# Eight GpSimd additions per group moved, and VectorE forms the rotation sums of three of the four groups

## The chip, the core and the metric

The kernel runs on one core of one Trainium2 chip. The metric is the device time of one execution in microseconds. Everything is float32. The median of three runs of the kernel before is 1265.38 us (1263.79 to 1267.1).

## The reference

A two-layer decoder over x of 8 batches x 256 tokens x 256 features. The first layer is attention with 16 heads, cross attention on a context of 120 rows and a mixture of 8 experts, each followed by a layer norm. The second layer, where the change lies, is a gated linear-style attention, a cross attention and a channel mix. Cut to what matters here:

```
x = _layernorm(x + L1_attn(x)); x = _layernorm(x + L1_xattn(x, ctx)); x = _layernorm(x + L1_ffn(x))

L1_attn:  xn = layernorm(x) * ln1_g + ln1_b
          q = l2norm(xn @ Wq); k = l2norm(xn @ Wk); v = xn @ Wv          # 16 heads of 16
          q = rope(q); k = rope(k)          # r1 = x1*cos - x2*sin ; r2 = x1*sin + x2*cos
          gcp = exp(clip(cumsum(-softplus(xn @ gate_w + gate_b)), -60, 50)); q *= gcp; k /= gcp + 1e-8
          p_exp = exp(p - max p) * softplus(xn @ clock_w + clock_b)      # p = xn @ p_w + p_b
          q /= cumsum(p_exp) + 1e-8; k *= p_exp
          out = softmax(causal(q @ k.T / 4)) @ v @ out_w + out_b
          x1 = out + x
          return x1 + gelu(layernorm(x1) @ mlp_w1 + mlp_b1) @ mlp_w2 + mlp_b2
```

## The kernel before

The 2048 tokens are worked in four groups (G = 4) of two batches: 512 tokens, NT = 4 tiles of 128 partitions x 256 features. The last part of the kernel, `last_layers`, is a pipeline over periods p = 0 to 3 and an end. In period p, group a = p is in the front stage (norms, projections, gates, rotation, causal attention), group r = p - 1 in the middle stage (output product, MLP), and group z = p - 2 in the rear (cross attention and channel mix). Each engine has its own list of instructions, written out by hand in order; an instruction waits only on the semaphores named before it. So an instruction that waits holds back all that stands behind it on its engine. Group 0 is alone in period 0, and its front stage is done in halves. In the trace period 0 lies at 745 to 834 us, period 1 at 834 to 925, period 2 at 925 to 1038.5, period 3 at 1038.5 to 1151.

The steps that the change touches:

- **Rotation.** VectorE `rotate` (line 2723) multiplies a 128x512 tile of queries and keys in PSUM by cos into `ra` (line 2725) and crosswise by sin into `rb` (line 2731), and signals `turning`. GpSimd adds the two (line 1572, for group 0 line 1546, 128x512) and signals `swung`. VectorE waits for `swung` (line 2974) and scales the sum by the inverse norms (line 2976), after which TensorE turns it (line 1769).
- **What VectorE does behind each tile's rotation** in periods 1 to 3: behind tile 0 the clock product (line 2940, 128x1024), behind tile 1 the product with the exponentials (line 2947), behind tile 2 four running sums (line 2672), behind tile 3 a small maximum (line 2959). Each comes right behind a drain.
- **Bias rows.** `add_rows` (line 1492) adds a bias row to four tiles on GpSimd (line 1495, 128x256 each): eight additions per group, four that fill `x1` and signal `biased0`, four in place. Before the change they stand behind the gather of the next group's expert rows and wait for `qkt`, the last of the `factors` (lines 2680 and 2683).
- **add_rest** (line 1521, 128x1024) and the clock sum (line 1567, 128x1024; line 1543 in halves for group 0), both on GpSimd.
- **Attention loop.** For every quad of heads q = 0 to 7: TensorE `scores` (line 1692), VectorE `minimum` twice (line 2746, on PSUM), ScalarE exponentials twice (line 2297), TensorE `weighted` (line 1703). Between the minimums VectorE does, for q = 1 to 4, `combine` twice (line 2625, 128x256, on the gathered expert rows of the next group) and statistics. For group 0 one `combine` follows each of the last eight minimums.

Of the kernel before, what the change touches and what calls it, by code (L numbers as in the profile page):

```python
# [8 lines left out]
ALU = mybir.AluOpType  # L9
# [11 lines left out]
NT = GT // P  # L21
# [1277 lines left out]
def last_layers(nc, dram, memory, keep):  # L1299


    with ExitStack() as ctx:
# [24 lines left out]
        HALF = NT // 2  # L1327
# [67 lines left out]
        def x(g, t):  # L1395

            return keep["x"][:, NT * g + t, :]
# [29 lines left out]
        def gates_of(g):  # L1427

            return g + 1 if g else 0
# [52 lines left out]
        def _(pool):  # L1482
# [9 lines left out]
            def add_rows(g, r, out):  # L1492

                for t in range(NT):
                    last = pool.tensor_tensor(out(t), x(g, t), brow[:, r, :], ALU.add)  # L1495
                return last
# [22 lines left out]
            def add_rest(g):  # L1519

                pool.tensor_tensor(keep["x"][:, bass.ts(g, NT), :], keep["x"][:, bass.ts(g, NT), :], x1[:, :, :], ALU.add).then_inc(biased1, 1)

            def rstd(g, n, b):

                h = slice(HALF * b, HALF * b + HALF)
                pool.wait_ge(n.stats, 2 * g + b + 1)
                pool.tensor_tensor(n.var[:, h], n.mv[:, h, 1], eps[:, h], ALU.add)  # L1527
                pool.drain()
                pool.tensor_tensor(n.inv[:, h], n.var[:, h], minus_half[:, 0, h], ALU.pow).then_inc(n.rstd, 1)  # L1529
# [8 lines left out]
            front_rstd(0, 1)  # L1538
            constants()
            pool.wait_ge(rows, NR * 16)  # L1540
            for b in range(GB):
                pool.wait_ge(uready, b + 1)
                pool.tensor_tensor(csum[:, :, batch(b)], csum[:, :, batch(b)], clog[:, :, batch(b)], ALU.add).then_inc(clogged, 1)
                for t in range(NT)[rows_of(b)]:
                    pool.wait_ge(turning, t + 1)
                    pool.tensor_tensor(firstrb[:, t, :], firstrb[:, t, :], firstra[:, t, :], ALU.add).then_inc(swung, 1)
            pool.wait_ge(vmm, NT)
            gather(1)
            pool.wait_ge(n4.normed, NT)
            pool.wait_ge(qkt, NT)  # L1550
            add_rows(0, 0, lambda t: x1[:, t, :]).then_inc(biased0, 1)
            add_rows(0, 1, lambda t: x(0, t))
            front_rstd(1, 0)
            front_rstd(1, 1)
            for p in range(1, PERIODS):
                a, r, z = stages(p)
                if z is not None:
                    pool.wait_ge(n6.turned, 2 * z + 2)
                    add_rows(z, 2, lambda t: x(z, t)).then_inc(biased2, 1)
                if r is not None:  # L1560
                    rstd(r, n5, 0)
                    rstd(r, n5, 1)
                    if z is not None:
                        add_rest(r)
                if a is not None:
                    pool.wait_ge(uready, gates_of(a) + 1)
                    pool.tensor_tensor(csum[:, :, :], csum[:, :, :], clog[:, :, :], ALU.add).then_inc(clogged, 1)
                    for t in range(NT):
                        if z is not None and t == NT - 1:
                            rstd(z, n7, 0)  # L1570
                        pool.wait_ge(turning, NT * a + t + 1)
                        pool.tensor_tensor(rb[:, t, :], rb[:, t, :], ra[:, t, :], ALU.add).then_inc(swung, 1)
                if r is not None and z is None:
                    add_rest(r)
                if z is not None:
                    rstd(z, n7, 1)
                    pool.wait_ge(n7.copied, 2 * z + 2)
                    columns = x5t[:, :, :, :].rearrange("p k b s -> p (k b) s")
                    pool.tensor_tensor(rl[:, :, :].rearrange("p k (b s) -> p (k b) s", b=GB), columns[:, :, 1:S + 1], columns[:, :, 0:S],
                                       ALU.subtract).then_inc(apart, 1)  # L1580
                if a is not None and a + 1 < G:
                    pool.wait_ge(vmm, NT * a + NT)
                    gather(a + 1)
                if a is not None:
                    pool.wait_ge(n4.normed, NT * a + NT)
                    pool.wait_ge(qkt, NT * a + NT)
                    add_rows(a, 0, lambda t: x1[:, t, :]).then_inc(biased0, 1)
                    add_rows(a, 1, lambda t: x(a, t))
                    if a + 1 < G:
                        front_rstd(a + 1)  # L1590
                if r is not None:
                    rstd(r, n6, 0)
                    rstd(r, n6, 1)
                if z is not None:
                    rstd(z, n8, 0)
                    rstd(z, n8, 1)
# [1019 lines left out]
        def _(dve):  # L2616
# [106 lines left out]
            def rotate(g, t):  # L2723

                dve.tensor_tensor((ra if g else firstra)[:, t, :].rearrange("p (h d) -> p h d", d=HALF1),
                                  bank[qk_bank(g, t)][:, :].rearrange("p (h d) -> p h d", d=HALF1),
                                  rope[:, t % 2:t % 2 + 1, 0:HALF1].to_broadcast([P, 64, HALF1]), ALU.mult)
                q4 = bank[qk_bank(g, t)][:, :].rearrange("p (h two d) -> p h two d", two=2, d=HALF1)
                r4 = (rb if g else firstrb)[:, t, :].rearrange("p (h two d) -> p h two d", two=2, d=HALF1)
                for o in range(2):  # L2730
                    last = dve.tensor_tensor(r4[:, :, o, :], q4[:, :, 1 - o, :],  # L2731
                                             rope[:, t % 2:t % 2 + 1, HALF1 * (1 + o):HALF1 * (2 + o)].to_broadcast([P, 32, HALF1]), ALU.mult)
                last.then_inc(turning, 1)

            def square_sums(g, t):

# [168 lines left out]
            for p in range(1, PERIODS):  # L2905
# [59 lines left out]
                if a is not None:  # L2965
                    dve.drain()
                    dve.wait_ge(lsum, gates_of(a) + 1)
                    dve.tensor_tensor(qfac[:, :, :], qfac[:, :, :], gsum[:, :, :], ALU.add).then_inc(qsum, 1)
                    dve.drain()
                    dve.wait_ge(ginv, gates_of(a) + 1)  # L2970
                    dve.tensor_tensor(pexps[:, :, :], pexps[:, :, :], gabs[:, :, :], ALU.mult)
                    dve.wait_ge(rnr, gates_of(a) + 1)
                    for t in range(NT):
                        dve.wait_ge(swung, NT * a + t + 1)
                        part = rb[:, t, :].rearrange("p (h d) -> p h d", d=DH1)
                        dve.tensor_tensor(part, part, rn[:, t * 32:(t + 1) * 32].unsqueeze(2).to_broadcast([P, 32, DH1]),  # L2976
                                          ALU.mult).then_inc(roped, 1)
# [251 lines left out]
```

## Time and profile before

| what | value |
|---|---|
| median of three runs | 1265.38 us |
| the profiled execution | 1264.11 us |
| its span in the trace | 1262.4 us |
| granted TensorE clock, mean | 0.961 of full |
| GpSimd busy over the span | 457.1 us (36%) |
| VectorE busy over the span | 750.2 us (59%) |

Times in the rows are microseconds from the span's start, unless marked ns. Line numbers are those of the kernel. DVE is VectorE, ACT ScalarE, PE TensorE (its matmuls), POOL GpSimd. In rows of the timeline the first number is the start, the second the time to the end of the merged instructions; a bracket holds the engine's idle time just before and what ended it.

### The profile page before, as it was taken

How to read it: one execution, taken by the hardware profiler on the slowest of the kernel's cores; microseconds unless marked ns; L12 is line 12 of the kernel's file. 1: busy time of each engine (PE TensorE's matmuls, PEld its weight loads, DVE VectorE, ACT ScalarE, POOL GpSimd, SP SyncE). 2: the span in 40 equal slices, each digit the busy share in tenths (PEclk: the TensorE clock that was granted, in tenths of full speed). 3: DMA queues.
4: the chain of work that ended last, by engine and by line, in shares of the span. 5: the costliest groups of instructions: out<-in, count | busy, mean ns of one | idle time of the engine just before them, and what ended most of it. 6: DMA issues, size and time to landing. Idle time of an engine off the chain costs nothing. (4 is left out here: it accounts for less than half of the span.)

```text
span 1262.4 us, 20442 instructions
## 1 busy us (share of the span) xinstructions
PE 1113.0 (88%) x6750; PEld 789.2 (63%) x6750; DVE 750.2 (59%) x2260; ACT 548.3 (43%) x1411; POOL 457.1 (36%) x539
## 2 busy tenths in 40 slices
PE   7899988998899798699999948579798999999996
PEld 3466455644564467599999945345565575566774
DVE  1383367236724764455556546749849885966366
ACT  1372237124612552233333317457566556744541
POOL 0151026003500575566666642503523613222022
PEclk9999999999999999699999988669999999999999
DMA  6000020020002004571111114100100100000001
GB/s 198 17 2 1 18 57 2 1 55 19 2 1 57 1 2 132 199 252 52 43 51 52 48 53 141 34 1 1 34 9 1 34 2 25 1 1 25 1 1 34
DMA packets 40228, 52.38 MB, mean 41 GB/s; under 512 B 10780, under 2 KB 33372, under 8 KB 40124
## 3 DMA queue, kind: packets, MB, share of 16 engines
q1 hardware_dynamic: 31100, 36.66, 9.1%
q0 software_dynamic: 3408, 9.31, 2.7%
q10 hardware_dynamic: 5616, 5.11, 1.2%
q8 instruction: 55, 0.90, 0.3%
q14 instruction: 49, 0.40, 0.1%
HBM read 41.76 MB, written 9.31 MB: 40 GB/s over the span
## 5 line engine op out<-in xcount | busy, mean ns | idle before, releaser
L1637 PE MATMUL bank<-words 128*128 128x256 f32 (+3 forms) x872 | 267.6, 457 | 13.3 <-DVE words L3048 2.4
L1637 PEld LDWEIGHTS bank<-words 128*128 128x128 f32 (+1 forms) x872 | 162.1, 193 | 92.4 <-issue 56.7
L419 PE MATMUL bank<-words 128*128 128x512 f32 x384 | 173.1, 602 | 8.4 <-DMA words<-in_wq 8.4
L371 POOL TENSOR_TENSOR words<-words 128x256 f32<-128x256 f32 (+1 forms) x128 | 103.4, 829 | 176.2 <-DVE words L972 176.2
L1182 PEld LDWEIGHTS bank<-words 128*128 128x128 f32 x1248 | 147.4, 194 | 3.5 <-ACT words L1216 1.6
L1182 PE MATMUL bank<-words 128*128 128x128 f32 x1248 | 147.9, 277 | 0.9 <-ACT words L1216 0.9
L754 ACT ACTIVATE words<-words 128x128 f32<-128x128 f32 (+1 forms) x256 | 113.3, 444 | 50.7 <-DVE words L967 50.7
L419 PEld LDWEIGHTS bank<-words 128*128 128x128 f32 x384 | 72.5, 193 | 90.7 <-issue 90.1
L706 ACT ACTIVATE words<-bank 128x512 f32<-128x512 f32 x48 | 28.7, 598 | 192.6 <-PE bank L419 192.6
L1231 ACT ACTIVATE words<-words 128x1024 f32 x39 | 41.1, 1057 | 145.1 <-PE bank L1182 128.4
L808 DVE COPY words<-bank 128x512 f32<-128x512 f32 x48 | 33.1, 690 | 106.3 <-PE bank L419 106.1
L963 DVE CUSTOM_DVE_ANT_0 words<-bank,words 128x128 f32<-128x128 f32 (+1 forms) x256 | 76.0, 353 | 20.4 <-PE bank L430 18.8
L1193 PE MATMUL bank<-words 128*128 x312 | 73.9, 380 | 0.7 <-DVE words L1280 0.7
L443 PE MATMUL bank<-words 128*128 128x128 f32 x384 | 55.8, 282 | 16.8 <-DVE words L983 9.1
L430 PE MATMUL bank<-words 64*128 64x128 f32 (+1 forms) x512 | 58.9, 351 | 8.6 <-DVE words L967 5.2
L1527 POOL TENSOR_TENSOR words<-words 128x2 f32<-128x2 f32 x32 | 7.0, 219 | 162.7 <-DVE words L2655 162.6
L443 PEld LDWEIGHTS bank<-words 128*128 128x128 f32 x384 | 41.7, 143 | 37.8 <-issue 26.6
L456 PE MATMUL bank<-words 128*64 128x256 f32 (+1 forms) x512 | 55.8, 337 | 10.1 <-ACT words L762 9.1
L983 DVE COPY words<-bank 128x768 f32<-128x768 f32 x64 | 59.6, 931 | 7.4 <-PE bank L443 7.4
L1138 POOL COPY words<-words 128x1024 f32 x39 | 40.3, 1035 | 60.7 <-PE bank L1182 60.7
L2297 ACT ACTIVATE words<-bank 128x768 f32<-128x768 f32 x64 | 48.9, 812 | 30.3 <-DVE bank L2746 30.3
L1193 PEld LDWEIGHTS bank<-words 128*128 128x128 f32 x312 | 56.2, 190 | 7.1 <-issue 1.1
(347 smaller groups left out, 2006.7 us busy)
## 6 DMA issues: line engine op xcount, KB each, us to landing
words<-in_w SPq DMA_DIRECT2D x8, 1024.0 KB, 9.5
y_slots<-words ACTq DMA_DIRECT2D x39, 128.0 KB, 1.7
words<-in_w SPq DMA_DIRECT2D x8, 512.0 KB, 10.1
words<-in_xt SPq DMA_DIRECT2D x4, 512.0 KB, 4.1
words<-in_x SPq DMA_DIRECT2D x4, 512.0 KB, 4.2
x_rows<-words SPq DMA_DIRECT2D x16, 128.0 KB, 1.8
words<-in_wm SPq DMA_DIRECT2D x2, 1024.0 KB, 6.6
out_x<-words SPq DMA_DIRECT2D x16, 128.0 KB, 1.8
```

Of the source, the lines that this page charges most:

```text
L371: last = pool.tensor_tensor(part, part, inv[:, j % SLOTS0, :, t:t + 1].to_broadcast([P, 2, P * (t + 1)]), ALU.mult)
L419: last = pe.matmul(bank[c % 2][:, :], w, r, start=k == 0, stop=k == KD - 1)
L430: last = pe.matmul(bank[SCORES[i % 2][n]][:, t * P:t * P + P * (t + 1)],  kt[r, m, b * S + t * P:b * S + (t + 1) * P], qt[r, m, b * S:b * ...
L443: last = pe.transpose(bank[2 + n][:, k * P:(k + 1) * P], prob[:, j % SLOTS0, n, c:c + P], ident[:, :])
L456: last = pe.matmul(bank[4 + j % 2][DH0 * n:DH0 * n + DH0, queries], v[:, 2 * b + k, h * DH0:(h + 1) * DH0], probt[:, j % 2, n, probs_of], ...
L754: last = act.activation(prob[:, i % SLOTS0, n, c], prob[:, i % SLOTS0, n, c], ACT.Exp, bias=negmax[:, i % SLOTS0, n, t:t + 1], scale=DH0 * ...
L963: dve.tensor_tensor_reduce(out=prob[:, i % SLOTS0, n, c], in0=bank[SCORES[i % 2][n]][:, c], in1=mask0[:, c], scale=1.0, scalar=-3e38, op0= ...
L983: dve.tensor_copy(probt[:, j % 2, :, :], turned).then_inc(tcopied, 1)
L1182: last = pe.matmul(bank[(BANKG, BANKV)[half][j % 2]][:, c * P:(c + 1) * P], wfix[:, j % 2, k * 2 * FF + half * FF + c * P:k * 2 * FF + hal ...
L1193: last = pe.matmul(bank[BANKY[j % 2]][:, 0:D], hidden[:, j % 2, k * P:(k + 1) * P], w2[:, bass.ds(e * W2 + k * D, D)], start=k == 0, stop= ...
L1637: last = pe.matmul(out, w, r, start=i == 0, stop=i == len(pairs) - 1)
L2297: act.activation(es[:, j % 4, :, :], pair(j % 2)[:, :, 0:CAUSAL], ACT.Exp, scale=DH1 ** -0.5).then_inc(s1e, 1)
```

## The change

Group 0: its eight bias additions move ahead of the clock sums and rotation sums; they wait for `n4.normed` alone. Groups 1 to 3: the four additions `rb + ra` leave GpSimd. VectorE makes each itself behind the tile's rotation, with a drain ahead of it, and its waits for `swung` go. The clock sum waits also for the last normalised rows of the middle group (`n5.normed`). In period 1 `add_rest` comes right behind the clock sum. The gather waits for all four `turning` signals, which the removed loop waited for until then. The eight bias additions are spread over the attention loop: two after the minimums of each of the quads q = 1 to 4.

```diff
             pool.wait_ge(rows, NR * 16)
+            pool.wait_ge(n4.normed, NT)
+            add_rows(0, 0, lambda t: x1[:, t, :]).then_inc(biased0, 1)
+            add_rows(0, 1, lambda t: x(0, t))
             for b in range(GB):
...
             gather(1)
-            pool.wait_ge(n4.normed, NT)
-            pool.wait_ge(qkt, NT)
-            add_rows(0, 0, lambda t: x1[:, t, :]).then_inc(biased0, 1)
-            add_rows(0, 1, lambda t: x(0, t))
...
                     pool.wait_ge(uready, gates_of(a) + 1)
+                    pool.wait_ge(n5.normed, NT * r + NT)
                     pool.tensor_tensor(csum[:, :, :], csum[:, :, :], clog[:, :, :], ALU.add).then_inc(clogged, 1)
-                    for t in range(NT):
-                        if z is not None and t == NT - 1:
-                            rstd(z, n7, 0)
-                        pool.wait_ge(turning, NT * a + t + 1)
-                        pool.tensor_tensor(rb[:, t, :], rb[:, t, :], ra[:, t, :], ALU.add).then_inc(swung, 1)
-                if r is not None and z is None:
-                    add_rest(r)
+                    if z is None:
+                        add_rest(r)
+                    if z is not None:
+                        rstd(z, n7, 0)
...
                 if a is not None and a + 1 < G:
                     pool.wait_ge(vmm, NT * a + NT)
+                    pool.wait_ge(turning, NT * a + NT)
                     gather(a + 1)
                 if a is not None:
                     pool.wait_ge(n4.normed, NT * a + NT)
-                    pool.wait_ge(qkt, NT * a + NT)
-                    add_rows(a, 0, lambda t: x1[:, t, :]).then_inc(biased0, 1)
-                    add_rows(a, 1, lambda t: x(a, t))
+                    for q in range(1, NT + 1):
+                        pool.wait_ge(s1m, PAIRS1 * a + 2 * q + 2)
+                        for t in (2 * (q - 1) % NT, 2 * (q - 1) % NT + 1):
+                            if q <= HALF:
+                                last = pool.tensor_tensor(x1[:, t, :], x(a, t), brow[:, 0, :], ALU.add)
+                            else:
+                                pool.tensor_tensor(x(a, t), x(a, t), brow[:, 1, :], ALU.add)
+                        if q == HALF:
+                            last.then_inc(biased0, 1)
...
                 last.then_inc(turning, 1)
+                if g:
+                    dve.drain()
+                    dve.tensor_tensor(rb[:, t, :], rb[:, t, :], ra[:, t, :], ALU.add)
...
                     for t in range(NT):
-                        dve.wait_ge(swung, NT * a + t + 1)
                         part = rb[:, t, :].rearrange("p (h d) -> p h d", d=DH1)
```

## Rows read from the trace of the kernel before

**Rows 1.** The page: busy time, share of the span and instructions of each engine.

```profile
PE 1113.0 (88%) x6750; PEld 789.2 (63%) x6750; DVE 750.2 (59%) x2260; ACT 548.3 (43%) x1411; POOL 457.1 (36%) x539
```

**Rows 2.** Busy time by stage: window, its length, engines, granted clock, DMA share, GB/s.

```profile
745.00:834.00 89.00, 55.01 (x356) 36.59 (x360) 59.73 (x120) 44.84 (x88) 34.04 (x42) 0.71 0.24 74
...
925.00:1038.50 113.50, 107.08 (x673) 68.94 (x672) 84.59 (x174) 70.10 (x144) 37.03 (x43) 0.98 0.05 12
```

**Rows 3.** Chain that ended last, 750 to 925: start, us, what.

```profile
817.16 3.64 DVE words L2625
```

**Rows 4.** Groups by line and form from 745 us on: busy us, mean ns, idle.

```profile
L2940 DVE TENSOR_TENSOR words<-words 128x1024 f32<-128x1024 f32 x3 | 7.0, 2338 | 0.3
...
L2959 DVE TENSOR_SCALAR words<-words 128x128 f32<-128x128 f32 x3 | 4.0, 1339 | 0.3
L2971 DVE TENSOR_TENSOR words<-words 128x1024 f32<-128x1024 f32 x3 | 3.7, 1226 | 0.3
...
L2835 DVE TENSOR_TENSOR words<-words 128x512 f32<-128x512 f32 x2 | 1.4, 694 | 0.2
...
L1572 POOL TENSOR_TENSOR words<-words 128x512 f32<-128x512 f32 x12 | 15.2, 1269 | 54.0 <-DVE words L2731 54.0
```

**Rows 5.** Timeline, VectorE, period 2: the running sums alone and beside a GpSimd addition.

```profile
954.50 2.42 DVE L2672 TENSOR_TENSOR_SCAN words<-words 128x256 f32<-128x256 f32 x4
...
974.76 3.55 DVE L2672 TENSOR_TENSOR_SCAN words<-words 128x256 f32<-128x256 f32 x4
```

**Rows 6.** Timeline, period 0: GpSimd, VectorE and TensorE around the bias additions.

```profile
815.04 5.47 POOL L1495 TENSOR_TENSOR words<-words 128x256 f32<-128x256 f32 x8
...
817.07 3.73 DVE L2625 SCALAR_TENSOR_TENSOR words<-words 128x256 f32<-128x256 f32 x1
...
822.31 1.65 PE L1692 MATMUL bank<-words 32*128 32x256 f32 x8 [2.60 <-ACT words L2297]
```

**Rows 7.** Timeline, VectorE, period 0: where the additions go, and its idle gaps.

```profile
768.95 1.27 DVE L2809 TENSOR_TENSOR_SCAN words<-words 128x256 f32<-128x256 f32 x2 [6.46 <-ACT words L2336]
...
771.53 0.74 DVE L2817 TENSOR_REDUCE words<-words 128x1 f32<-128x256 f32 x2 [0.80 <-ACT words L2324]
...
782.98 1.27 DVE L2809 TENSOR_TENSOR_SCAN words<-words 128x256 f32<-128x256 f32 x2 [0.66 <-ACT words L2336]
...
786.39 0.83 DVE L2853 TENSOR_TENSOR words<-words 128x512 f32<-128x512 f32 x1 [0.86 <-ACT words L2372]
```

**Rows 8.** Timeline, period 1: the attention loop, VectorE and TensorE.

```profile
899.34 0.41 DVE L2645 TENSOR_TENSOR words<-bank,words 128x256 f32<-128x256 f32 x1
...
900.51 3.60 DVE L2625 SCALAR_TENSOR_TENSOR words<-words 128x256 f32<-128x256 f32 x2
...
905.72 1.03 DVE L2625 SCALAR_TENSOR_TENSOR words<-words 128x256 f32<-128x256 f32 x2
...
906.81 0.94 PE L1692 MATMUL bank<-words 32*128 32x256 f32 x16 [2.83 <-ACT words L2297]
...
911.45 1.30 DVE L2746 TENSOR_TENSOR bank<-bank,words 128x512 f32<-128x512 f32 x2 [0.89 <-PE bank L1692]
```

**Rows 9.** Timeline, period 1: VectorE and GpSimd around the clock sum and add_rest.

```profile
858.38 4.55 DVE L2672 TENSOR_TENSOR_SCAN words<-words 128x256 f32<-128x256 f32 x4
...
883.21 2.00 POOL L1521 TENSOR_TENSOR words<-words 128x1024 f32<-128x1024 f32 x1
...
883.43 2.86 DVE L2968 TENSOR_TENSOR words<-words 128x1024 f32<-128x1024 f32 x1
```

**Rows 10.** Timeline, period 2: VectorE and TensorE, the normal order and the loop.

```profile
951.67 2.27 DVE L2702 TENSOR_SCALAR words<-words 128x8 f32<-128x8 f32 x1
...
990.71 4.19 DVE L2976 TENSOR_TENSOR words<-words 128x512 f32<-128x512 f32 x4
...
993.23 3.17 PE L1769 MATMUL bank<-words 128*128 128x128 f32 x16 [2.05 <-DVE words L2976]
...
1018.16 1.30 DVE L2746 TENSOR_TENSOR bank<-bank,words 128x512 f32<-128x512 f32 x2
```

## The prediction, made before the change was run

> **What bounds the kernel now.** I read the page first, then the busy times by stage, then the chain of work that ended last, and last the timelines of VectorE and GpSimd side by side. TensorE is busy for 88% of the span [rows 1], but not evenly: 55.0 of 89 us in period 0, at a granted clock of 0.71, and 107.1 of 113.5 us in period 2, at 0.98 [rows 2]. The change touches only work of VectorE and GpSimd, so it can only count where TensorE waits for them. The chain shows one such place at 817 us: a single `combine` of group 0 holds it for 3.64 us [rows 3]. There TensorE stands still for 2.60 us ahead of the next scores [rows 6]; in period 1 it stands still for 2.83 us behind two `combine` that took 3.60 us [rows 8], and in period 2 for 2.05 us until the scaled rotation is there [rows 10].
>
> **One mechanism explains all three places.** A VectorE instruction whose two inputs both lie in SBUF, or a plain TENSOR_SCALAR in SBUF, stands still for as long as a GpSimd addition runs. The 128x1024 product of line 2940 takes 2338 ns when line 1572 (1269 ns) starts with it, and the same shape at line 2971 takes 1226 ns [rows 4]: it pays 1.11 us. The four running sums take 2.42 us alone and 3.55 us beside an addition [rows 5]. A maximum over 128x128 takes 1339 ns [rows 4]. An instruction that reads PSUM pays nothing: line 2645 keeps its 0.41 us in the midst of the bias additions [rows 8]. And additions back to back give nothing away in between: the `combine` that began at 817.07 ended only when the run of eight (815.04, 5.47 us) was over [rows 6].
>
> The Trainium skill, page "SBUF — State Buffer", section "SBUF: two separate sides", calls the shared pair of ports an exclusive lock for the whole instruction. The rows agree, and go further, since several additions in a row kept VectorE out. That rule also speaks against two edits of this change, which put GpSimd additions beside `combine` and beside the running sums.
>
> **Rotation sums (groups 1 to 3).** Removed: 12 additions on GpSimd, each met by a VectorE instruction. Added on VectorE: 12 additions of 128x512, for which line 2835 stands (694 ns [rows 4]), and a drain, taken as 0.09 us, the usual gap in the timeline: 0.78 us. The trade per tile: tiles 0 and 1 each 1.11 - 0.78 = 0.33 us gained, tile 2 3.55 - 2.42 - 0.78 = 0.35, tile 3 about 1.17 (1.27 less the little that the maximum needs) - 0.78 = 0.39. Together 1.4 us per group. The bounds of an addition with its drain: 0.6 us, if the drain is hidden, to 1.36, if it takes what GpSimd took; that is 2.1 us gained to 0.9 lost per group. I take 0.78, since the row is the same operation, shape and memory. In periods 2 and 3 this chain ends in line 2976, for which TensorE waits [rows 10]. GpSimd's difference for the channel mix still meets line 2976 there (4.19 us [rows 10]), before as after. TensorE itself and ScalarE stand close behind this chain, so 0.4 us of the 1.4 is certain and the rest needs the GELUs to come in time; I take 1.4.
>
> **Clock sum and add_rest.** In periods 2 and 3 the clock sum now waits for the last normalised rows. Line 2702 loses its 2.27 us stall [rows 10] and would start ScalarE 2 us sooner, but the running sums behind it, 2.42 us now [rows 5], meet the same addition and become the 4.55 us of period 1 [rows 9]. That is 2.1 saved and 2.1 paid on VectorE: nothing. What is queued behind the new wait on GpSimd has no earlier use. In period 1 `add_rest` (2.00 us) leaves line 2968, which pays 2.86 - 1.23 = 1.63 us for it [rows 4, 9], and stands right behind the clock sum. If a run of additions keeps the lock, as in rows 6, the last running sum waits 2.0 us more; if VectorE gets in between, only the reduction follows, and nearly nothing is paid. By the skill's sentence ("held for the full instruction") VectorE would get in between, and period 1 would be 1.7 us better than I sum. I take 2.0. Period 1 ahead of its loop: -1.4 - 1.6 + 2.0 = **-1.0 us**. The gather's extra wait costs nothing: those signals were awaited before too; its eight indirect DMAs now start earlier in period 1, where add_rest stood ahead of them, and nowhere later.
>
> **Bias additions, period 1.** Two `combine` fall from 3.60 to 1.03 us [rows 8]. Two of the additions (1.4 us, a quarter of 5.5) are now released after the minimums of quad 1 and run until 0.35 us into that pair: 2.57 - 0.35 = 2.2 us gained. At quads 2 and 3 the pair follows the minimum at once and loses 1.4 us; VectorE idles 0.89 us before the next minimum [rows 8], the other 0.5 us lies in part under ScalarE's head copies. I take 0.4 us for the period; bounds 0 and 4.2 (three full collisions). Net **-1.8 us**. Period 1 in all: -2.8.
>
> **Bias additions, periods 2 and 3.** Before, they ran ahead of quad 0 beside VectorE's PSUM work and cost nothing. Now they meet `combine` in period 2, where the minimum of quad 3 follows with no idle time ahead of it [rows 10]. In odd quads TensorE has 2 us more of MLP work to hide a late minimum, in even ones not. I take +0.5, bounds 0 and 4.2. Period 3 has no `combine`: 0. So period 2 gives -1.4 + 0.5 = **-0.9**, period 3 **-1.4**.
>
> **Bias additions, group 0.** The `combine` at 817 us no longer meets them; TensorE's gap there is 2.60 us [rows 6], so 2.6 gained (bounds 2.2 and 3.3). But they now run behind the masks, from about 765.4 us, and take 5.47 us [rows 6], until 770.9. The first running sums start at 768.95 [rows 7] and wait 2.0 us; the clock sum, 1.27 us as line 1572 has for that shape [rows 4], then falls on them too: 3.3 us late. VectorE idles 0.80, 0.66 and 0.86 us on the way [rows 7], 2.3 in all. That leaves 1.0 (bounds 0 and 3.3). Net **-1.6**.
>
> **Sum.** -1.6 - 2.8 - 0.9 - 1.4 = -6.7 us. The span of 1262.4 becomes 1255.7, the profiled execution 1264.11 becomes 1257.4. That execution lies 1.3 us under the median, so the median 1265.38 becomes **1258.7 us**, 0.53% less. About 0.3%, or 3.8 us, is what a measurement of this kernel can tell from no change.
>
> **Rivals.**
> 1. *VectorE gets the lock between the clock sum and add_rest, and loop collisions are hidden.* For it: slack before most minimums. Against it: the 3.73 us row. It gives -6.7 - 1.7 - 0.9 = -9.3: 1256.1. Chance 0.17.
> 2. *Only part arrives.* In periods 2 and 3 TensorE and ScalarE were the late ones, so only 0.4 of 1.4 counts in each (+2.0), and group 0 pays 2.3 instead of 1.0 (+1.3): -3.4, or 1262.0. For it: TensorE is busy 107.1 of 113.5 us in period 2 [rows 2]. Chance 0.2.
> 3. *The change doesn't do what it says*: an addition with its drain costs VectorE 1.2 us, no less than the stall it replaces. 12 x 0.42 = 5.0 us back: -1.7, or 1263.7. Against it: the drain was there already behind `rotate`, so there is one addition more and one drain more. Chance 0.08.
> 4. *Slower: the bias additions in the loop set its pace.* Ten pairs (eight beside `combine` in periods 1 and 2, two beside `mix_result`, line 2753, in period 3) would each delay the next minimum by 1.4 us with nothing to hide it: 14.0, of which 0.9 is in my sum, so -6.7 + 13.1 = +6.4, or 1271.8. It decides from six such delays on (my gain without loop costs is 7.6 us). For it: the missing idle time at 1018 us [rows 10]. Against it: the 0.89 us of idle time in period 1 [rows 8]. Chance 0.05.
> 5. *The clock.* In period 0 the granted clock averages 0.71 [rows 2], between its two levels, 1.2 and 2.4 GHz. Period 0 loses a gap of 2.6 us in the scores; full clock may come back sooner or later by a few us. That widens each case by 1.5 us and is counted in them.
>
> My forecast has 0.5.
>
> **How the numbers follow.** Predicted is the likeliest case, 1258.7. The range runs from 1254.6 (rival 1 less 1.5) to 1263.8 (rival 2 with the clock against it, and rival 3 at its middle); it leaves out rival 4, half of rival 3 and the tails, some 0.15 to 0.2. Faster by over 0.3% means below 1261.6: nearly all of the forecast, all of rival 1 and 0.4 of rival 2, 0.73. Within 0.3%: the rest of rival 2, rival 3 and a little of the forecast, 0.21. Slower: rival 4 and a tail, 0.06.
>
> **What would show it.** Lines 2940 and 2947 should fall to about 1.2 us each, the sums behind tile 2 to 2.4, line 2959 to about 0.2, and three groups of four new additions of 0.6 to 0.7 us should stand behind line 2731. Line 2702 should fall to 0.2 and line 2672 ahead of the rotation rise to 4.4 in periods 2 and 3. The `combine` at 817 should take 0.5 and TensorE's gap of 2.83 in period 1 go to about 0.6. If the running sums at 858 us take 6.5 us, add_rest kept the lock. If line 2625 in the loop takes over 2.4 us a pair and gaps before line 1692 grow by as much, rival 4 is at work. If TensorE's gap before line 1769 grows while VectorE is early, rival 2 is.

## The result

| | median | against the kernel before |
|---|---|---|
| before | 1265.91 us (1262.52 to 1267.29, 6 runs) | |
| changed kernel | 1260.40 us (1259.52 to 1262.64, 6 runs) | 0.9959 (95%: 0.9945 to 0.9973) |
| the same program, second measurement | 1253.79 us | 0.9897 (0.9883 to 0.9912) |
| third measurement | 1259.05 us | 0.9958 (0.9944 to 0.9973) |
| fourth measurement | 1252.96 us | 0.9888 (0.9870 to 0.9906) |

The forecast of 1258.7 us lies 1.7 us from the first measurement. But the same program gains 0.4% in two measurements and 1.1% in two others, so more went on than the sum knew. The profiled execution of the first measurement is 1260.94 us, its span 1259.1 us.

First the page of the changed kernel, engine by engine (busy us, share, instructions); it answers [rows 1].

```profile
PE 1114.4 (89%) x6750; PEld 791.2 (63%) x6750; DVE 744.2 (59%) x2272; ACT 548.9 (44%) x1411; POOL 445.3 (35%) x527
```

Twelve instructions have left GpSimd (539 to 527) and twelve came to VectorE (2260 to 2272), yet VectorE's busy time fell by 6.0 us: it was "busy" standing still. The groups by line and form of VectorE show where (busy us, mean ns | idle); they answer [rows 4].

```profile
L2740 DVE TENSOR_TENSOR words<-words 128x512 f32<-128x512 f32 x12 | 8.3, 694 | 1.1
L2947 DVE TENSOR_TENSOR words<-words 128x1024 f32<-128x1024 f32 x3 | 3.7, 1226 | 0.2
L2954 DVE TENSOR_TENSOR words<-words 128x1024 f32<-128x1024 f32 x3 | 3.7, 1226 | 0.2
L2966 DVE TENSOR_SCALAR words<-words 128x128 f32<-128x128 f32 x3 | 0.7, 228 | 0.2
```

Line 2740 is the new addition, 694 ns as the row of line 2835 had promised. Line 2947 (before: 2940) fell from 2338 to 1226 ns, line 2966 (before: 2959) from 1339 to 228 ns.

Period 1 in the timeline, VectorE, GpSimd and TensorE; it answers [rows 8, 9].

```profile
859.43 4.55 DVE L2676 TENSOR_TENSOR_SCAN words<-words 128x256 f32<-128x256 f32 x4
...
860.78 2.65 POOL L1567 TENSOR_TENSOR words<-words 128x1024 f32<-128x1024 f32 x1 [2.04 <-ACT words L2433]
863.39 2.38 POOL L1521 TENSOR_TENSOR words<-words 128x1024 f32<-128x1024 f32 x1
...
865.16 0.63 DVE L2938 TENSOR_SCALAR words<-words 128x4 f32<-128x4 f32 x1
...
900.28 1.31 DVE L2629 SCALAR_TENSOR_TENSOR words<-words 128x256 f32<-128x256 f32 x2
...
904.29 0.93 PE L1696 MATMUL bank<-words 32*128 32x256 f32 x16 [0.54 <-ACT words L2301]
```

The running sums take 4.55 us, as before, though `add_rest` (line 1521) follows the clock sum (line 1567) at once: VectorE got in between, and only line 2938 pays 0.46 us (0.63, where it took 0.17 before). The pair of `combine` takes 1.31 us where it took 3.60, and TensorE's gap of 2.83 us is 0.54.

Group 0 in the timeline of the changed kernel; it answers [rows 6, 7]:

```profile
766.42 6.47 POOL L1495 TENSOR_TENSOR words<-words 128x256 f32<-128x256 f32 x8 [0.26 <-issue]
...
769.61 1.90 DVE L2816 TENSOR_TENSOR_SCAN words<-words 128x256 f32<-128x256 f32 x2 [6.41 <-ACT words L2340]
...
815.61 0.94 POOL L1489 DMA_INDIRECT words<-y_slots,words  x1 [0.30 <-issue]
816.96 0.42 DVE L2684 TENSOR_TENSOR words<-bank,words 128x256 f32<-128x256 f32 x1 [3.77 <-remote]
...
821.89 0.47 DVE L2629 SCALAR_TENSOR_TENSOR words<-words 128x256 f32<-128x256 f32 x1
```

The `combine` of 3.73 us takes 0.47, as forecast. But a wait has appeared that no part of the change makes: line 2684 stands for 3.77 us, and begins 0.41 us after the last indirect DMA has been issued (815.61 + 0.94). I call it the **stand**. In the trace of before the same instruction (line 2680) waits 0.74 us.

Period 2 and the end, VectorE and TensorE of the changed kernel; they answer [rows 10]:

```profile
949.21 0.17 DVE L2706 TENSOR_SCALAR words<-words 128x8 f32<-128x8 f32 x1
...
949.94 4.54 DVE L2676 TENSOR_TENSOR_SCAN words<-words 128x256 f32<-128x256 f32 x4
...
987.19 4.19 DVE L2982 TENSOR_TENSOR words<-words 128x512 f32<-128x512 f32 x4
...
990.24 1.86 PE L1773 MATMUL bank<-words 128*128 128x128 f32 x12 [1.35 <-DVE words L2982]
...
1236.55 3.41 PE L1641 MATMUL bank<-words 128*128 128x256 f32 x8 [2.22 <-DVE words L3047]
```

The last row is no part of the change: the same eight matmuls took 1.97 us in the trace of before, after the same idle time of 2.22 us:

```profile
1241.49 1.97 PE L1637 MATMUL bank<-words 128*128 128x256 f32 x8 [2.22 <-DVE words L3041]
```

Its stretch (window, length, busy time of the engines, granted clock, DMA share, GB/s) in the changed kernel:

```profile
1236.00:1241.00 5.00, 4.45 (x15) 3.68 (x16) 3.13 (x8) 0.33 (x1) 0.81 (x2) 0.66 0.00 0
```

and the same work in the kernel before:

```profile
1241.00:1246.00 5.00, 4.13 (x20) 3.34 (x20) 3.39 (x8) 1.43 (x3) 1.80 (x2) 1.00 0.00 0
```

A granted clock of 0.66 (between 1.2 and 2.4 GHz) against 1.00, with the same gap ahead: this execution lost 1.4 us in those eight matmuls, and 1.7 us of the span there, for no reason that the rows tell apart. A second such stretch is 1075 to 1083 us (granted clock 0.79; the kernel before has 1.00 in 1077 to 1085).

**Where the time went, by stage.** Between two traces I compare the start of the same ScalarE instruction. The difference (other trace less the one of before) stays flat where both kernels run alike and steps where they don't. The steps, in us, with stages in the time of before:

| trace | ahead of 760 | group 0, to 845 | period 1, to 925 | period 2, to 1040 | period 3, to 1150 | to 1250 |
|---|---|---|---|---|---|---|
| changed, first | +0.7 | +0.3 | -3.5 | -1.6 | -0.6 | +1.4 |
| e1_again | -1.2 | -3.1 | -4.4 | -1.6 | -1.6 | -0.3 |
| e6_again | -0.2 | 0.0 | -3.5 | -1.6 | -1.6 | -0.3 |
| e11_again | +2.0 | -4.9 | -2.8 | -1.6 | -0.6 | +1.2 |
| e5_before_copy | -0.3 | +0.1 | +1.2 | +0.2 | +1.0 | +0.1 |
| e2_rotation_only | +1.0 | -1.5 | -3.3 | -1.2 | -1.5 | +1.4 |
| e3_bias_only | +0.7 | -3.2 | -2.2 | +0.2 | +1.0 | +0.1 |
| e4_group0_only | +2.6 | -4.3 | +1.1 | +0.2 | +0.1 | +1.8 |
| e9_run_behind_wait | +1.0 | -0.8 | -1.9 | +1.0 | +0.3 | +0.1 |
| e12_no_n5_wait | +1.1 | -4.5 | -4.3 | -1.5 | -1.2 | -0.3 |

How much of a step means nothing is seen in e5 (the kernel before itself) and in group 0 of e2 (nothing of the change there, and yet -1.5): single stages differ by up to about 1.5 us from one trace to the next. The trace of before is also short in period 1: e4 and e5, which leave that period as it was, need 1.1 and 1.2 us more there.

### The profile page after: what moved, and what is told of

It is laid out like the page before. It is cut to its first block and busy times, and to the rows that moved or that the text cites. A ratio compares the mean times of both kernels' runs of the same rounds, so it can differ in the third digit from the quotient of the medians.

```text
span 1259.1 us, 20455 instructions
## 1 busy us (share of the span) xinstructions
PE 1114.4 (89%) x6750; PEld 791.2 (63%) x6750; DVE 744.2 (59%) x2272; ACT 548.9 (44%) x1411; POOL 445.3 (35%) x527
```

## The experiments

Four kernels each ran on one chip: e1 to e4, e5 to e8, e9 to e12. Each of the three chips was used once. Which chips the two first traces came from is not on record.

**The change itself, three times more, and the kernel before itself.**

> The changed kernel itself, once more. Its first trace has a stand of VectorE in the second half of group 0: the instruction at 816.96 us begins 3.77 us after what it needs is there, and scores follow 3.3 us later than they would. It also has a lower granted clock in 1075 to 1083 us (0.79) and in 1236 to 1241 us (0.66) than the kernel before had in the same work. Theory A: the stand belongs to this kernel (its instruction stream on VectorE, or what runs beside the gather), so it is there again with 3 to 4 us, the drops of the clock too, and the ratio to the kernel before is 0.9955 to 0.9965 again. Theory B: it was a matter of that execution, the stand is under 1 us this time, the profile's span is some 3 us shorter (1256), and the median stays at 1260.4, because the timed executions never had it.

> The kernel before itself, loaded as one more kernel, to see how far the same program differs from one load to the next. So far the changed kernel has a ratio of 0.9959 in one measurement and 0.9897 in the next, with a trace that shows two stands of VectorE (3.77 and about 0.84 us) in the first and none in the second. Theory L (a load of a program can have such stands in all its executions, and most don't): ratio 1.000 within 0.002, no stand of VectorE over 0.7 us without a releaser. Rival (every load differs by some us, the kernel before too): ratio outside 0.998 to 1.002, and segments of the span that the change doesn't touch differ by over 2 us.

> The changed kernel for the third time. Theory L: no stand of VectorE in the trace, ratio 0.988 to 0.992 as in the second measurement; the first was the odd one. Rival (the first was the usual one): 0.995 to 0.997 with the stand at 817 us there again. By periods, against the trace of the kernel before: group 0 -3 us, period 1 -4.4, period 2 -1.6, period 3 -1.6.

> The changed kernel once more, to compare with the others of this call. With the stand of VectorE at 813 to 817 us: ratio 0.995 to 0.9965, since the kernel before hides its late combine behind the same stand and group 0 gains nothing. Without it: 0.989 to 0.991.

Measured: e1 0.9897, e6 0.9958, e11 0.9888, e5 1.0002 (0.9987 to 1.0016). The stand, first in the copy of the kernel before (e5), VectorE and GpSimd:

```profile
815.62 0.42 DVE L2680 TENSOR_TENSOR words<-bank,words 128x256 f32<-128x256 f32 x1 [3.70 <-remote]
...
818.36 5.87 POOL L1495 TENSOR_TENSOR words<-words 128x256 f32<-128x256 f32 x8 [3.06 <-DVE words L2683]
...
820.56 0.85 DVE L2625 SCALAR_TENSOR_TENSOR words<-words 128x256 f32<-128x256 f32 x1
```

Then the changed kernel on that chip (e6) and on the one before it (e1):

```profile
815.14 0.42 DVE L2684 TENSOR_TENSOR words<-bank,words 128x256 f32<-128x256 f32 x1 [3.72 <-remote]
```

```profile
812.04 0.43 DVE L2684 TENSOR_TENSOR words<-bank,words 128x256 f32<-128x256 f32 x1 [0.74 <-PE bank L1841]
```

The traces of all four kernels e5 to e8 have the stand (3.70, 3.72, 3.52, 3.69 us), none of e1 to e4 and e9 to e12 has it. So it comes neither with the change (theory A of e1) nor with one kernel of a group and not the next (theory L, whose expectation for e6 missed as well as the one that e5 would have no stand); theory B of e1, that the timed executions were free of it, fell too. It comes with the group of four, that is with the chip or with the occasion: each chip was used once, so these two can't be told apart.

The rows explain a part of the difference between the two ratios. **Without the stand** the moved additions take away the `combine` of 3.7 us: group 0 gains 3.1 us in e1. **With the stand** they take away nothing: VectorE signals the last factors 3 us later, so in the kernel before the additions begin at 818.36, behind a wait, and the `combine` takes 0.85 us (the first three together pay 1.1 us). The kernel before hides its own collision behind the stand (e5: group 0 +0.1), the changed one just has the stand (e6: 0.0). Period 1 has a smaller one, 0.84 us in the first trace (TensorE idle 0.83 us ahead of the scores at 896.90) and about as much in e6, but not in e1. Between e1 (-13.6 us) and e6 (-4.8 us) lie 8.8 us; the two stands are 3.1 and 0.9 us of them. No row accounts for the other 4.8.

**The parts alone.**

```diff
 # e2_rotation_only against before: groups 1 to 3
-                        pool.tensor_tensor(rb[:, t, :], rb[:, t, :], ra[:, t, :], ALU.add).then_inc(swung, 1)
+                    pool.wait_ge(turning, NT * a + NT)
...
+                if g:
+                    dve.drain()
+                    dve.tensor_tensor(rb[:, t, :], rb[:, t, :], ra[:, t, :], ALU.add)
...
-                        dve.wait_ge(swung, NT * a + t + 1)
```

> The kernel before with the rotation sums of groups 1 to 3 on VectorE and nothing else changed: the bias additions, add_rest and the clock sum keep their places. Theory (as predicted): 1.4 us per group where VectorE's chain sets the time. In period 1 that is -1.4 and add_rest still stands beside the squares of line 2968, at no gain; in period 2 -1.4, in period 3 -0.6 to -1.4; together -3.4 to -4.2, so 1262 +- 0.7. The clock sum now falls on the running sums or on line 2702 as before. Rival (TensorE and ScalarE were the late ones in periods 2 and 3): -1.4 in period 1 and -0.2 to -0.4 in the others, -2.0 in all, 1263.8. Rival (an addition with its drain costs VectorE 1.2 us): -0.5 or nothing, 1265.

> The kernel before with the bias additions moved (group 0's behind the masks, those of groups 1 to 3 spread over the quads of the loop), and nothing else: the rotation sums, add_rest and the clock sum stay as they were. Theory (by the trace of the changed kernel): group 0 gains the combine at 817 us, -3.3 less 0.1 to 1.0 for the running sums at 769 us; period 1 gains the pair of combines, -2.2 to -2.5; the collisions in the loops of periods 1 and 2 cost 0.1 to 0.5 together. That is -4.5 to -5.5, 1260 to 1261. If the stand of VectorE beside the gather of group 0 comes with the moved additions, the same trace shows it here too, and the gain falls to -1.5 to -2. Rival (the loop's collisions pace it, 1.4 us each): +5 or more.

> The kernel before with group 0's bias additions alone moved from behind qkt to behind the masks. Theory: the combine at 817 us takes 0.5 instead of 3.73 us, TensorE's gap of 2.60 us is gone, and the early additions cost 0.1 to 1.0: -1.6 to -3.2 us, 1262.5 to 1264. Rival 1: VectorE stands still beside the gather for 3 to 4 us because the additions no longer run there or because its stream has moved: then nothing is left, 1265 to 1266. Rival 2: the running sums at 769 us wait for the whole run of additions and pass it on in full: -1 at most.

e3's and e4's edits are those of the diff above for the bias additions, all of them and group 0's alone. Measured, on the chip without the stand:

| | ratio | median less before's 1267.39 |
|---|---|---|
| e1, all | 0.9897 (0.9883 to 0.9912) | -13.6 us |
| e2, rotation sums | 0.9935 (0.9922 to 0.9947) | -8.2 us |
| e3, bias additions | 0.9937 (0.9924 to 0.9950) | -7.5 us |
| e4, group 0's of them | 0.9963 (0.9950 to 0.9976) | -4.7 us |

By the medians each part gives more than expected. How much of that is the part's own is open: the kernel before has 1267.39 us on this chip and 1265.91 in the first measurement, and no trace of it was taken here. e2 and e3 together are 15.6 us, the whole is 13.6: 2.0 us are counted twice. The intervals of the three are 1.6 us wide to each side, so the medians alone don't settle that. The stages do: in period 1, against e4's +1.1, e2 gains 4.4, e3 3.3 and e1 5.5 us, 2.2 us less than the two parts. The timeline of e2 shows which. GpSimd and VectorE in period 1:

```profile
895.70 5.90 POOL L1495 TENSOR_TENSOR words<-words 128x256 f32<-128x256 f32 x8 [1.33 <-DVE words L2682]
```

```profile
880.48 2.53 DVE L2735 TENSOR_TENSOR words<-words 128x512 f32<-128x512 f32 x1
...
898.98 1.34 DVE L2624 SCALAR_TENSOR_TENSOR words<-words 128x256 f32<-128x256 f32 x2
```

With the bias additions in their old place and in the midst of them, the pair of `combine` takes 1.34 us, not 3.60. That gain of 2.3 us, which I had booked on spreading the additions, comes from the rotation part as well: GpSimd is early, has to wait for the last factors (1.33 us), and this run lets VectorE in. The first row of VectorE tells of `add_rest`: in e2 it waits for the fourth `turning` signal and so starts with the fourth new addition, which takes 2.53 instead of 0.69 us. The changed kernel avoids that at a price of 0.46 us (line 2938) and 0.28 us of a longer wait for ScalarE; what is left is the 1.1 us by which period 1 is better in e1 than in e2.

**When a run of GpSimd additions keeps VectorE out.**

```diff
 # e9_run_behind_wait against before; group 0 likewise with s1m >= 1
                     pool.wait_ge(qkt, NT * a + NT)
+                    pool.wait_ge(s1m, PAIRS1 * a + 4)
                     add_rows(a, 0, lambda t: x1[:, t, :]).then_inc(biased0, 1)
```

> The kernel before with one wait more ahead of each run of eight bias additions: in group 0 for its first minimum, in groups 1 to 3 for the fourth minimum of the group. The additions stay in one run, and now lie wholly beside combines. In the traces so far, eight additions that begin straight behind the last indirect DMA took 5.47 to 5.51 us and the combine beside them stood until their end (3.73, 3.75, 3.60 us), while eight that began behind a wait took 5.87 to 5.90 us and the combines beside them took 0.65 to 1.03 (one) and 1.34 (two). Theory W (a run keeps VectorE out only where it begins without a wait): the run takes 5.8 to 6.5 us in both places, the combines beside it cost 0.2 to 0.5 us each, and the kernel gains what the moved additions gain: group 0 -2.5 to -3 where VectorE doesn't stand beside the gather, period 1 -2; -3.5 to -5 in all there, and -1.5 to -2.5 on a chip where it does stand. Rival (the prediction's: a run of additions keeps the lock, whatever is ahead of it): one combine stands for 4 to 5.4 us in each group, and the kernel is 1 to 3 us slower than before.

Measured: 0.9971 (0.9960 to 0.9983), 3.0 us less than before. Group 0 first, where the new wait had long been fulfilled when GpSimd came to it (the loop of the first batch had signalled it), then period 1, where it waited:

```profile
815.53 5.49 POOL L1495 TENSOR_TENSOR words<-words 128x256 f32<-128x256 f32 x8
...
899.83 6.26 POOL L1495 TENSOR_TENSOR words<-words 128x256 f32<-128x256 f32 x8 [1.85 <-DVE bank L2748]
```

```profile
817.56 3.74 DVE L2627 SCALAR_TENSOR_TENSOR words<-words 128x256 f32<-128x256 f32 x1
...
900.73 1.66 DVE L2627 SCALAR_TENSOR_TENSOR words<-words 128x256 f32<-128x256 f32 x2
```

Period 1 came out as theory W said: the run takes 6.3 us, and the pairs beside it 1.66 and 1.50 us, 0.6 and 0.5 us over their 1.03. Group 0 came out as the rival said: 5.49 us, and one `combine` of 3.74 us that ends with the run. So a wait in the program is not enough; this one had been fulfilled and changed nothing. The runs that kept VectorE out all stand behind indirect DMAs without a pause: group 0 of before, e2 and e9, period 1 of before, e4 and e5. Each took 5.47 to 5.51 us, and the `combine` beside it ended with the run. Runs with a pause ahead let VectorE in: e2 and e9 in period 1 (1.33 and 1.85 us of idle time ahead), e9 in period 2 (8.03 us; the run takes 5.96 us), e5 in group 0 (3.06 us).

The early run of the changed kernel (766.42 us) is a third case, and it decides what the condition is not. It has 0.26 us of idle time ahead of it and waits for nothing that the profile shows, yet it takes 6.47 us and the running sums get in after 0.63 us (1.90 instead of 1.27). So a wait that really waits isn't needed either. What the runs that keep VectorE out have in common, and the others lack, is that they stand straight behind GpSimd's indirect DMAs. Whether the DMAs ahead do it or the missing pause, no run separates. The length of a run alone tells nothing of this. In period 3 of the kernel before, eight additions behind a real wait took 5.52 us, because VectorE read PSUM there and had nothing to get in with:

```profile
1115.03 5.52 POOL L1495 TENSOR_TENSOR words<-words 128x256 f32<-128x256 f32 x8 [9.86 <-DVE words L2683]
```

One added wait thus gives 1.9 us in period 1. The 2.5 to 3 us expected of group 0 are missing because it did not wait there, so the whole stays under the expected 3.5 to 5. In period 2, where the run now lies beside `combine` and before did not, two pairs pay 0.3 and 0.5 us and the stage loses 1.0.

**The price of an addition.**

```diff
 # e8_second_addition against the changed kernel
                     dve.tensor_tensor(rb[:, t, :], rb[:, t, :], ra[:, t, :], ALU.add)
+                    dve.drain()
+                    dve.tensor_tensor(ra[:, t, :], rb[:, t, :], ra[:, t, :], ALU.add)
```

> The changed kernel with a second addition of 128x512 and a second drain on VectorE behind each of the 12 rotation sums (its result goes to a buffer that is no longer read): the price of one addition with its drain on this chain. Theory: 0.7 to 0.8 us each, all on the path: period 1 +3.0, periods 2 and 3 +3.0 each less what TensorE and ScalarE hide there (0 to 1 us each): +7 to +9.3 against the changed kernel of this call. Rival 3 of the prediction (1.2 us): +12 to +14. Rival 2 (VectorE isn't what periods 2 and 3 wait for): period 1 +3.0 and the others under +1.5 each, +4 to +6.

```profile
882.56 0.69 DVE L2740 TENSOR_TENSOR words<-words 128x512 f32<-128x512 f32 x1
883.33 0.69 DVE L2742 TENSOR_TENSOR words<-words 128x512 f32<-128x512 f32 x1
884.09 0.25 DVE L2968 TENSOR_SCALAR words<-words 128x128 f32<-128x128 f32 x1
...
895.60 1.30 DVE L2755 TENSOR_TENSOR bank<-bank,words 128x512 f32<-128x512 f32 x2 [3.08 <-remote]
```

From one addition to the next it is 0.77 us, the 0.78 of the sum. The median is 11.5 us above e6's. Twelve additions make 9.2; the other 2.3 us lie in period 1 (5.4 us worse than e6's, four additions are 3.1). The last row there is a second stand, beside the gather of that period: 3.08 us where e6 has 1.94, so it gives 1.1 of the 2.3 us. The rest was not followed up. Periods 2 and 3 are 3.1 and 3.7 us worse: what is added to VectorE counts there in full (3.1 us of additions a period), and rival 2 has no place left. Rival 3, an addition of 1.2 us, is out by the 0.77.

**Edits that gave nothing.**

```diff
 # e12_no_n5_wait against the changed kernel
-                    pool.wait_ge(n5.normed, NT * r + NT)
```

> The changed kernel without the clock sum's new wait for the normalised rows. Theory (as predicted): periods 2 and 3 pay either way. Line 2706 takes 2.2 us again instead of 0.17 and line 2676 behind it 2.4 instead of 4.5; no difference to the changed kernel of this call, 0 +- 0.5 us. Rival: the wait lets ScalarE start 2 us sooner and the kernel gains from it, so that without it the kernel is 1 to 4 us slower.

Measured 1253.06 us, e11 beside it 1252.96. The medians alone allow some 3 us either way; the stages are closer, with -1.5 and -1.2 us in periods 2 and 3 against e1's -1.6 and -1.6. In period 2 of e12:

```profile
943.95 2.28 DVE L2705 TENSOR_SCALAR words<-words 128x8 f32<-128x8 f32 x1
...
946.78 2.43 DVE L2675 TENSOR_TENSOR_SCAN words<-words 128x256 f32<-128x256 f32 x4
```

The stall of 2.1 us goes back to the small instruction and the sums are free: the wait moves it and saves nothing.

```diff
 # e7 against the changed kernel, beside group 0's rotation sums on VectorE
-                    pool.tensor_tensor(rl..., columns[:, :, 1:S + 1], columns[:, :, 0:S], ALU.subtract).then_inc(apart, 1)
+                    dve.tensor_tensor(rl..., columns[:, :, 1:S + 1], columns[:, :, 0:S], ALU.subtract).then_inc(apart, 1)
```

> The changed kernel, and on VectorE as well the rotation sums of group 0 and the channel mix difference of periods 2 and 3 (GpSimd's line 1576, which line 2982 meets). Theory (the same mechanism): the scaled rotation of line 2982 takes 4.19 us beside the difference, and alone 4 products of about 0.65 = 2.7, less the difference itself on VectorE (128x1024 in two pieces or one, about 1.3 us by the 1226 ns of the 128x1024 product): -0.2 to +0.1 a period; group 0 gains the stalls of its four sums less 0.78 each, about -1 where VectorE sets the pace there. In all -0.5 to -1.5 against the changed kernel of this same call. Rival: VectorE already has no slack in periods 2 and 3, so the difference on it adds 1 us a period: +1 to +2.

```profile
987.12 2.58 DVE L2975 TENSOR_TENSOR words<-words 128x512 f32<-128x512 f32 x4
989.62 1.26 DVE L2980 TENSOR_TENSOR words<-words 128x1024 f32<-128x1024 f32 x1
```

The scaled rotation falls from 4.19 to 2.58 us and the difference costs 1.26: the terms are as expected, but they leave only 0.35 us a period. The median is 1259.49 against 1259.05 us of e6: no gain is seen, and the 0.5 to 1.5 us expected did not come.

```diff
 # e10_gather_late against the changed kernel, group 0
             pool.wait_ge(vmm, NT)
+            pool.wait_ge(qkt, NT)
             gather(1)
```

> The changed kernel with group 0's eight indirect DMAs behind qkt, so that they are issued from about 815 us on and not from 805 us. On some chips VectorE's line 2684 stood 3.5 to 3.8 us there, until the last of the eight had been issued. Theory (the stand comes from the issues of the gather): on a chip where the changed kernel shows it (see the copy of it in this call), it is gone from line 2684 here; either nothing takes its place (-3 us against that copy), or an instruction of the loop behind 815 us stands instead until the last issue at about 825 us, and nothing or less than nothing is gained. Rival (it comes from the place in VectorE's instruction stream alone): line 2684 stands here as well, and the time is that of the copy. On a chip without the stand: no difference, 0 +- 1 us.

Measured 0.9948 (0.9928 to 0.9968), 6.9 us above e11. The experiment failed. Its chip has no stand, and the edit made a wait of its own: four `combine` wait for their gathered rows.

```profile
821.30 0.48 DVE L2630 SCALAR_TENSOR_TENSOR words<-words 128x256 f32<-128x256 f32 x1 [1.49 <-DMA words<-y_slots,words]
```

So it says nothing about the cause of the stand. It does say that this gather can't be 12 us later without loss.

## Why the prediction was right, and where it only looks right

**The mechanism** was right in its core. Every stall beside a GpSimd addition that the sum took away is gone, with the forecast durations: 1226 and 228 ns, 0.17 for line 2706, 4.54 for the sums ahead of the rotation, 0.47 for the `combine` of group 0, TensorE's gap 0.54 (forecast 0.6). How additions in a row share with VectorE, the forecast had wrong (below).

**Rotation sums.** 0.77 us for an addition with its drain (0.78). Forecast 1.4 us a period; e2 has 1.2 and 1.5 in periods 2 and 3; the changed kernel 1.6 in both, in e1 and e6, and 0.6 in period 3 of the first trace, where the granted clock of 0.79 at 1075 us costs 1.3. That all of it would arrive was put down as uncertain; it does (e2, e8).

**Clock sum and add_rest.** "Nothing" for periods 2 and 3 was right (e12). For period 1 "additions back to back give nothing away in between" was the step that failed: I paid 2.0 us, the row shows 0.46. I had drawn a rule from one row, the 3.73 us of group 0. It holds for runs straight behind the DMA issues and for no other run in the traces. The Trainium skill, page "SBUF — State Buffer", section "SBUF: two separate sides", has the pair of ports taken "for the whole instruction"; by that rule VectorE gets in between two additions. The rows agree for `add_rest` and for the early run; the 3.73, 3.74 and 3.75 us of the runs behind DMAs differ from it.

**Bias additions, period 1.** Forecast 2.2 less 0.4. The pair gains 2.3, and the pairs beside additions take 1.31 to 1.34 us against 1.03: 0.3 us each, of which next to nothing reaches TensorE. The place of the gain was right; that it needed the spread was not. It is the 2.2 us that e2 and e3 share. A question that would have found it: ask of each edit what it does to the start of the instructions that another edit also moves.

**Bias additions, period 2.** +0.5 forecast; nothing paid (-1.6 with, -1.2 to -1.5 from the rotation alone). Rival 4 asked for six delays of 1.4 us; none occurred. With that both halves of rival 1 came true, VectorE between the clock sum and `add_rest` and collisions that stay hidden. It had a chance of 0.17, and its mechanism describes the runs better than the forecast's own.

**Group 0.** Forecast 2.6 gained and 1.0 paid. Without the stand 3.1 us are gained net in e1 (3.2 to 4.9 in the other traces, with the stage's noise of 1.5): the `combine` gives its full 3.3 (the upper bound), and the early additions cost under 0.1 in e1. In the first trace the sums that wait take 1.90 instead of 1.27 us, line 2818 0.73 instead of 0.43 and line 2830 1.51 instead of 0.68, 1.8 us in all, and 2.3 us of idle time absorb that; my 3.3 assumed that the run kept the lock. With the stand the group gains nothing. That case was in none of the rivals.

**The sum.** -6.7 forecast. Without the stand the stages from 760 us on give -3.1 - 4.4 - 1.6 - 1.6 - 0.3 = -11.0 in e1, and the medians -13.6 and -13.3 us. Of the rest, 1.1 us is period 1 of the kernel before itself, by e4, which leaves that period as it was; for what remains there is no trace of before on those chips. With the stand the medians give -5.5 and -4.8. The first number came near by luck: two misses partly cancel there, period 1 with 0.7 us more than forecast and group 0 with nothing instead of 1.6. Where the stand is missing, 1253.8 and 1253.0 us lie below my range, and the gains of 13.6 and 13.3 us are twice the forecast and more than rival 1's 9.3. The range, made from one trace of before, had no term for that; the stages explain 11.0 of it in e1.

What stays open: what the stand comes from. In group 0 it ends 0.32 to 0.41 us after the last indirect DMA is issued in four traces (e5, e6, e8, the first of the changed kernel) and 0.80 us after it in e7. In period 1 that doesn't hold: the small stand of the first trace ends before the last issue,

```profile
893.33 1.30 DVE L2753 TENSOR_TENSOR bank<-bank,words 128x512 f32<-128x512 f32 x2 [1.90 <-PE bank L1696]
...
893.87 0.95 POOL L1489 DMA_INDIRECT words<-y_slots,words  x1 [0.30 <-issue]
```

and e8's at 895.60 us ends 1.5 us after it. So a link with GpSimd's DMA work is only argued; e10, made to test it, ran where the stand doesn't occur. A late delivery of VectorE's instructions is a rival that no run tests; in 15 us around that point the DMA queues carry one 16 KB piece of instructions in the first trace and one in e1, so they don't decide it. The Trainium skill, page "SBUF — State Buffer", section "SBUF: two separate sides", says that "Engine ports and AXI ports are disjoint"; by that a transfer as such would not stop VectorE's instruction. No run here settles that.

## What to carry to other kernels

Price an addition moved off GpSimd by the row of the same shape on VectorE, and count as gain the whole stall of the instruction that it used to meet. Before two edits are added up, look at whether both move the start of the same GpSimd work; here either alone removed the same 2.3 us. If GpSimd additions must stand beside VectorE's two-input work, don't put them straight behind GpSimd's indirect DMAs, since such a run shut VectorE out to its end; behind a wait that really waited, or behind other work, VectorE got in. And measure a gain more than once and on more than one chip: one program gave 5.5 and 13.6 us here.

## What the runs showed of the hardware that was not expected

- Eight additions of 128x256 on GpSimd straight behind indirect DMAs keep a VectorE instruction with two SBUF inputs out until the run ends, 5.47 to 5.51 us after it began (one `combine` took up to 3.75 us). With a pause of 0.26 to 8.03 us ahead, the run lets VectorE in, which pays 0.2 to 0.7 us each time, and itself takes 5.87 to 6.47 us.
- In some traces VectorE stood still for 3.5 to 3.8 us while GpSimd issued a gather, in the kernel before as in the changed one (four of four kernels on one chip, none of eight on two others). It can hide the gain of an edit beside it. The same program measured 0.9958 there and 0.9897 and 0.9888 elsewhere, of which the stands explain 4.0 of 8.8 us.
- After the same idle time of 2.2 us the granted clock was 0.66 in 1236 to 1241 us of the changed kernel's first trace and 1.00 in the same work of the kernel before. It cost 1.7 us there and 1.3 us at 1075 us.
